# A sandwich layer (scan and gated feed-forward) on eight cores: each Silu waits for its own chunk's matmuls

## The reference, cut to what matters

```python
# x: (8, 2048, 1024); one batch entry a core
x = x + layernorm(attn(layernorm(x)))      # attn: delta = softplus(x Wd), a scan over T with 16 states, times Wo
x = x + layernorm(ffn(layernorm(x)))

def ffn(x):                                 # inner size 4096
    gate = silu(bitlinear(x, w_gate))       # activations in 8 bits by row, weights ternary
    up = bitlinear(x, w_up)
    return bitlinear(gate * up, w_down)     # gate * up is quantized by row again
```

## Time and profile before

| what | value |
| --- | --- |
| median of 3 runs | 4117.7 us (4111.46 to 4128.93) |
| profiled execution, its own time | 4114.7 us |
| its span, slowest core (core 6) | 4112.9 us |
| spans of the other cores | 4090.7 to 4098.7 us |
| mean granted TensorE clock | 0.635 to 0.640 |
| TensorE, matmuls | 1310.0 us busy (32%) |
| VectorE | 1498.0 us busy (36%) |
| ScalarE | 1453.5 us busy (35%) |
| GpSimd | 267.8 us busy (7%) |

### The profile page before, as it was taken

One profiled execution on the slowest core, in us unless ns is written; L12 is line 12 of the kernel. 1 busy time (PEld: TensorE's weight loads), 2 busy tenths in 40 slices (PEclk: granted clock), 3 DMA queues, 4 the chain that ended last, 5 costly groups with the idle time before them and its releaser, 6 DMA issues.

```text
span 4112.9 us, 25485 instructions; the slowest of 8 cores (4090.7 to 4112.9 us)
## 1 busy us (share of the span) xinstructions
PE 1310.0 (32%) x5260; PEld 532.2 (13%) x5260; DVE 1498.0 (36%) x2016; ACT 1453.5 (35%) x2110; POOL 267.8 (7%) x443
## 2 busy tenths in 40 slices
PE   1121121200011112113644602644624626428463
PEld 0000000100000000001212200212202212103221
DVE  0015646389700000100457962357221477021500
ACT  2553544333344444455223333223033222131201
POOL 0001212123200000000111210000000000000000
PEclk9965555655555555555876655875667856659666
DMA  4042231100023222133310100310111301103111
GB/s 65 10 154 92 72 112 51 31 0 0 31 92 100 99 92 67 41 107 118 103 51 21 52 32 10 103 52 16 51 46 52 98 5 41 46 26 113 42 41 51
DMA packets 164345, 245.35 MB, mean 60 GB/s; under 512 B 6113, under 2 KB 121058, under 8 KB 160098
## 3 DMA queue, kind: packets, MB, share of 16 engines
q1 hardware_dynamic: 159906, 235.07, 17.2%
q0 software_dynamic: 4288, 8.65, 1.4%
HBM read 218.80 MB, written 33.55 MB: 61 GB/s over the span
## 4 chain that ended last, share of the span: by engine, by line
PE 24%; DVE 23%; ACT 22%; DMA 14%; issue 10%; POOL 6%; ACTq 1%; DVEq 1%; SPq 0%; POOLq 0%
DVE s_sig L289 10%; PE pD L991 7%; POOL s_state L263 6%; PE pG L867 5%; PE pU L875 5%; DMA s_td<-tdT 4%; DVE s_sig L296 4%; DMA wu_b<-wu 3%; DMA wg_b<-wg 3%; PE ptD L950 2%; ACT s_h L957 2%; PE pW L682 2%; DVE s_qs L899 2%; DMA wdn_b<-wdn 2%; DVE s_ytmp L313 1%
## 5 line engine op out<-in xcount | busy, mean ns | idle before, releaser
L282 ACT ACTIVATE s_abar<-s_dyq,s_nega 128x512 f32<-128x512 bf16 x512 | 369.4, 722 | 632.2 <-DVE s_sig L289 487.0
L289 DVE TENSOR_TENSOR_SCAN s_sig<-s_abar,s_state,s_lnf 128x512 bf16<-128x512 f32 x384 | 493.0, 1284 | 103.7 <-ACT s_abar L282 64.2
L991 PE MATMUL pD<-s_td,s_h 128*128 128x512 bf16 x1024 | 392.5, 567 | 217.6 <-DMA s_td<-tdT 214.0
L867 PE MATMUL pG<-s_tg,s_dyq 128*128 128x512 bf16 x1024 | 397.9, 389 | 162.4 <-DVE s_h L894 144.3
L875 PE MATMUL pU<-s_tu,s_dyq 128*128 128x512 bf16 x1024 | 397.5, 388 | 0.0
L263 POOL TENSOR_TENSOR s_state<-s_sig,s_onesp 128x1 bf16<-128x1 bf16 x384 | 249.2, 649 | 1699.0 <-ACT s_abar L282 912.4
L313 DVE SCALAR_TENSOR_TENSOR s_ytmp<-s_sig,s_bprm,s_ytmp 128x512 bf16<-128x512 bf16 x448 | 336.5, 751 | 48.2 <-DVE s_sig L289 1.4
L894 DVE TENSOR_TENSOR s_h<-s_gtmp,pU 128x512 bf16<-128x512 bf16 x128 | 88.0, 687 | 612.1 <-ACT s_gtmp L887 612.1
L887 ACT ACTIVATE s_gtmp<-pG,s_r1g 128x512 bf16<-128x512 f32 x128 | 88.0, 687 | 397.9 <-PE pU L875 228.6
L688 DVE TENSOR_TENSOR attnC<-pW,s_borep 128x512 f32<-128x512 f32 x16 | 11.1, 692 | 587.4 <-PE pW L682 587.1
L991 PEld LDWEIGHTS pD<-s_td,s_h 128*128 128x128 bf16 x1024 | 134.0, 135 | 475.2 <-issue 461.2
(11 more groups left out here) (155 smaller groups left out, 1705.6 us busy)
## 6 DMA issues: line engine op xcount, KB each, us to landing
wg_b<-wg SPq DMA_DIRECT2D x32, 1024.0 KB, 6.0
wu_b<-wu SPq DMA_DIRECT2D x32, 1024.0 KB, 5.6
wdn_b<-wdn SPq DMA_DIRECT2D x32, 1024.0 KB, 5.7
s_tg<-tgT SPq DMA_DIRECT2D x64, 512.0 KB, 3.4
s_tu<-tuT SPq DMA_DIRECT2D x64, 512.0 KB, 4.6
s_td<-tdT SPq DMA_DIRECT2D x64, 512.0 KB, 3.6
tgT<-wg_stage SPq DMA_DIRECT2D x16, 512.0 KB, 3.5
tuT<-wu_stage SPq DMA_DIRECT2D x16, 512.0 KB, 3.4
```

The source lines that it names most:

```text
L282: lambda h, d=dc, n_=n, p=pa: h.activation(out=s_abar[:, p, :], in_=delta_view[:, d, t0:t0 + QT], func=AF.Exp, scale=s_nega[:, d, n_:n_ + 1]),
L289: lambda h, d=dc, c_=col, p=pa, s=ps: h.tensor_tensor_scan(s_sig[:, s, :], s_abar[:, p, :], lnT_view[:, d, t0:t0 + QT], s_state[:, c_:c_ + 1],
L867: h.matmul(pGs[c_][:], q1T_view[:, k, t_ * 128:(t_ + 1) * 128], s_tg[:, wp, k4_, :], start=(k == 0), stop=(k == KC - 1)),
L991: lambda h, c_=c, k=kc, p=par, s_=sub, f=hf: h.matmul(pDs[c_][:, f * 512:(f + 1) * 512], q2T_view[:, c_, k, :], s_td[:, p, s_, f * 512:(f ...
```

## The change

Half 1's last matmul of every chunk gets an increment, not chunk 3's alone; half 0 keeps its one. The token after chunk c of half 1 is kept in `t_mm_c[c]`, and the Silu of chunk c waits for `t_mm_c[c]`. The tokens for the weight loads are the same places as before.

```diff
                     t_unit_mms = []
+                    t_mm_c = {}
...
-                                            inc=(1 if (c, k4) == (3, 3) else 0))
+                                            inc=(1 if (k4 == 3 and
+                                                       (half == 1 or c == 3)) else 0))
+                                if half == 1:
+                                    t_mm_c[c] = ST("tensor")
                             t_unit_mms.append(ST("tensor"))
-                        t_mm = t_unit_mms[-1]
                         for c in range(4):
...
                                     lambda h, t_=tc, c_=c, p=ppar: h.activation(
                                         out=s_gtmp[:, p, :], in_=pGs[c_][:], func=AF.Silu,
                                         scale=s_r1g[:, t_:t_ + 1]),
-                                    waits=([t_mm, ST("vector")] if c == 0
-                                           else [ST("vector"), sch.chain("scalar")]))
+                                    waits=([t_mm_c[c], ST("vector")] if c == 0
+                                           else [t_mm_c[c], ST("vector"),
+                                                 sch.chain("scalar")]))
```

## The result

The changed kernel takes 4028.81 us in the median of 8 runs (4020.22 to 4030.17), the kernel before 4117.04 us (4111.46 to 4131.22). The ratio is 0.9778, with a 95% interval of 0.9763 to 0.9792: faster by 2.2%. In a later comparison the ratio of the same two kernels was 0.9800 (0.9787 to 0.9814). The profiled execution has a time of 4024.73 us of its own; its slowest core is core 4.

A forecast was written before the change was run, and what follows sets the result against it. The kernel was taken as bound by engines waiting for each other, in gate/up TensorE and ScalarE in turn. 4114.7 - 78.8 + 3 gave 4038.9 us, 4041.9 from the median; stated 4040, range 4026 to 4072.

The forecast's parts named there:

- the sum of 78.8 us: Gate/up stages: Silus waiting for their own chunk save 58.4 us in groups 0 to 2 and 20.5 in group 3.
- load stalls: Gate/up weight loads, asked for more densely, sometimes land late and hold TensorE; 3 us taken off the gain.
- Boundaries and scan blocks: Gate/up stage: TensorE's gaps between successive oc close, group 3's end included (48.3 us); six scan blocks start 5.09 us earlier (30.5).
- My sentence that the level falls only after long waits: Gate/up stage: TensorE's clock drops to 1.2 GHz only behind long waits, which the change shortens; used against the slower-clock rival.
- The rival in which loads set the pace: Gate/up stages: nearly all weight loads take the long time, 27 us of stalls, 4063 us; chance 0.10.
- The lower edge of the range: 4026 us overall; the forecast's own range began at 4028, from the fastest run less the gain, 4033, less a few us.
- The clock rivals: TensorE in gate/up: lower level for half the matmuls, 4211 us, chance 0.03; or between levels, about 4118 us, chance 0.04.
- Increments, waits and evictions: Gate/up: three more increments an oc, one more wait before three Silus (bound 2.2 us), PSUM reads beside matmuls; taken as 0.

The follow-up runs named there:

- the second pair of profiles: The changed kernel profiled again without edit, set against the kernel with the increments alone; measured 4028.78 us against 4111.19, ratio 0.9800.

## Why the prediction was right or wrong

The mechanism was right, and what failed is the size of the gain: the sum of 78.8 us for the gate/up stages was too small, the 3 us taken off it for load stalls too large, and the stages outside stood at nothing. Forecast were 4040 us with a range of 4026 to 4072. The median, 4028.81, lies near its lower edge; by the ratio of that comparison, 0.9778 x 4117.04 = 4025.6, the time is just below it. The gain is 88 us by the medians and 91 by the ratio, where 76 were forecast. In the mean of the profiled cores it is 87.5 us: 82.0 from the gate/up stages, load stalls included, where 75.8 were forecast, and 5.5 from outside, which the second pair of profiles shows to be chance. Between the 87.5 and the 91 lies the choice of execution and core, which no run takes apart.

- *Boundaries and scan blocks.* Forecast 48.3 and 30.5 us; measured in the stages 50.4 and 31.5. The first boundary's 3.50 us gap is gone with its table load, the stage's short waits are gone, and the wait beside the block is 27.9 us where about 28 were forecast.
- *The sum of 78.8 us* was the first mis-sized term: it measured 82.0 and 81.2 in two pairs of profiles, with 0.9 us of load stalls already lost from the first. The rows shown were read rightly, but those of core 6's group 3 stood for all groups and cores: even core 6 itself gained 80.8 us, for some of its periods in groups 0 and 1 are 16.0 to 16.2 us. On half of the cores the kernel before lost 1 to 2 us more at the first boundary to the 1.2 GHz level, and a few periods were 0.2 to 0.4 us over 15.82. Averaged over the cores these make 1.0 us in group 0, 0.75 in group 2 and about 0.9 elsewhere, 2.6 of the missing 3.2. My sentence that the level falls only after long waits was wrong; core 6, from which it came, is one of the two cores that show no such fall.
- *The load stalls*, 3 us, were the second: the rows of waits show 0 to 2.8 us, 0.9 in the mean of the cores, beyond the first wait of the stage. The measured stages include them. The rival in which loads set the pace did not come.
- *The lower edge of the range* was the third. I had built it from the fastest run less the gain, and left nothing for the stages that the change does not touch. Their mean over the cores went 5.5 us down in one pair of profiles and 6.5 us up in the other.
- *The clock rivals.* Neither came. TensorE works with hardly a gap, and the granted clock of the changed kernel in group 3 of core 4 is 1.00, the 2.4 GHz level, at 94.93 us busy of 96:

```profile
3656.00:3752.00 96.00, 94.93 (x433) 42.91 (x441) 19.27 (x28) 19.23 (x28) 0.00 (x0) 1.00 0.49 158
```

Matmuls still start every 0.216 us, and the granted clock of all eight cores takes only the values 0.50 and 1.00, in every run. The Trainium skill, "TensorE: Matmul & The Clock Gate", section "Seeing it yourself", tells of a limiter that holds a die at 1.95 GHz once three of its cores run dense matmuls. The trace does not agree, and the measurement decides for this kernel and its data (activations rounded to whole numbers, weights of three values). One thing is assumed in this: each core's times count from its own first instruction, so that three cores of a die ran the stage at the same moment follows from their like spans only if they started together.

- *Increments, waits and evictions* were costed at nothing. The run with the increments alone confirms the first within its interval. Where TensorE comes last, the step from Silu 0 to Silu 1 is 1.78 us against 1.73 for the next; that may be the added wait, and no run tests it. All Silus and multiplies still take 686 to 690 ns, though most now run beside matmuls.

## What to carry to other kernels

A token taken with "the last thing listed so far" waits for more than the data needs. Three such tokens stood in this kernel: the last chunk for the first (2%), the last step of a scan block for a Silu (0.3%), and the step just listed for a load whose buffer was free one step before (6%). For each wait, ask which instruction last touched what is needed. Read the rows on more than one core, and take into the range what the untouched stages vary by; and before a saving is multiplied by the number of stages, look in each whether something else ends it.

## What the runs showed of the hardware that was not expected

TensorE's granted clock can fall around a short gap. Gaps are given here between two matmul starts. Of 128 gaps of 3.50 us in four profiles 34 were followed by 6 to 14 matmuls at the 1.2 GHz level. So were 14 of 40 gaps of 2.50 to 2.58 us, eight of them on all eight cores at the same place in one kernel, where the same gap in the kernel before was followed by none. None of 616 gaps of 2.22 us was. By the records the level fell between 0.95 us before TensorE resumed and 1.34 us after, so that some of the falls met an engine already back at 0.216 us a matmul. A fall cost up to about 3 us behind a gap of 3.50 us, and 1.7 us on the average of the eight cores behind the one of 2.57 us. One can't tell from a single core that it happens: core 6 of the kernel before shows none behind a short gap.
